# Seven quarter products for batch 1 as well, with the matrices for it prepared during batch 0

## The chip, the cores and the metric

One core of one Trainium2 chip runs the whole program. The time is that of the device, in microseconds (us), from start to end of one launch. TensorE (in the profile PE, its weight loads PEld) multiplies, VectorE (DVE) and ScalarE (ACT) work elementwise, GpSimd (POOL) does a little elementwise work, and SyncE (SP) issues nearly all transfers (DMA) from HBM.

## The reference

For each of 8 batches of 256 tokens (1024 channels), in float32:

```
w   = weight[adapter_ids[b]]              # 1024 x 1024, an adapter per batch
y   = x @ w.T                             # first product
out = x + y @ W_up.T + delta              # second product
# top1 = argmax(y @ gate_w.T + bias) over 4 experts
# delta = lora_B[top1] @ (lora_A[top1] @ y), rank 8
```

## The kernel before

**Numbers.** Each float32 operand is kept as a sum of two parts of lower precision, "hi" (ScalarE rounds, a CAST) and "lo" (VectorE subtracts hi from the raw number). A product is hi x hi + hi x lo + lo x hi: three matmuls.

**First product.** Per batch 8 blocks c of 128 output channels, block number n = 8b + c. TensorE runs block n into `ps_y[c % 2]`; ScalarE copies one half of it (`small`), VectorE adds the halves to `y_raw` (`y_full`). TensorE may begin block n only when `y_full` of block n - 2 is done. Meanwhile ScalarE and VectorE split W blocks ahead (`w_hi_part`, `w_lo_part`, three blocks ahead, `splits_at` and `splits_after` say which where), and SyncE loads W blocks into a ring of seven (`load_w`).

**Second product, in full.** Batches b < PLAIN = 2. y (256 x 1024) and W_up are each cut in four quarters; eight quarter products. The columns of lora_A and the gate ride along in the left quarters and give z and the logits. VectorE picks the expert (`choose`, a chain of small operations that ends in `z_parts`), TensorE transposes the result (`transpose_z`, ahead of the seventh of eight parts of the last quarter product), ScalarE copies it (`zT`), and TensorE adds the LoRA term (`add_lora`). VectorE adds the sums from PSUM onto the rows of x (`add_row`), and SyncE stores them.

**Second product, with seven quarter products.** Batches b >= PLAIN, by Strassen's scheme in Winograd's form: product 1 to 7 of sums of quarters of y (S1 to S4, by VectorE's `y_add`, split by `y_hi_part`, `y_lo_part`) with B11, B21, B22 and four sums of quarters of W_up, T1 to T4. These are made once: the raw quarters are copied from HBM again into the tiles `wide_stage` and `thin_stage`, summed (`t_raw`; the result stands in `wide_raw` or `thin_raw`), and split (`t_hi` on ScalarE, `t_lo` on VectorE). T1 and T4 are thin tiles, T2 and T3 wide ones. T4 uses the memory of B12, so its copies wait until the last product in full is done. In the kernel before T3 and T2 are summed in blocks 4 to 7 of batch 1's first product, T1 in its second, T4 in batch 2.

**Order.** There is no scheduler. Each engine has one program, written by hand, and runs it strictly in order; semaphores connect them. An instruction that waits holds up all behind it on its engine. SyncE's transfers too are issued in the program's order into one queue.

Of the kernel before, what the change touches and what calls it, by code (L numbers as in the profile page):

```python
# [8 lines left out]
ALU = mybir.AluOpType  # L9
# [16 lines left out]
def build(nc, xT, x, ids, w, w_up, gl, lora_b, bias, out):  # L26
# [22 lines left out]
    UNITS = 8  # L49
    PLAIN = 2  # L50
    QUART = HALF // 2
# [29 lines left out]
    with ExitStack() as ctx:  # L81
# [90 lines left out]
        up_ready = sem("up_ready")  # L172
        t_sum = sem("t_sum")
        t_hi_ready = sem("t_hi_ready")
        t_ready = sem("t_ready")
# [50 lines left out]

        T_ORDER = (T3, T1, T2, T4)

        def t_count(q, j):
            return 2 * T_ORDER.index(q) + j + 1  # L230

        SUM_ORDER = (T3, T2, T1, T4)

        def t_sum_count(q, j):
            return 2 * SUM_ORDER.index(q) + j + 1

        @block.sync
        def _(sp):
# [113 lines left out]
        @block.scalar  # L352
        def _(act):
# [23 lines left out]

            def t_hi(q):
                for j in range(2):
                    act.wait_ge(t_sum, t_sum_count(q, j))  # L380
                    act.copy(up_hi(q, pair(j)), up_raw(q, pair(j))).then_inc(t_hi_ready, 1)

# [25 lines left out]
            def first_product(b):  # L408
                for c in range(OC):
# [13 lines left out]
                    if (b, c) == (0, 5):  # L423
                        act.wait_ge(gl_in, 16)
                        gate_high(0)
                        gate_high(1)
                    if (b, c) == (1, 7):
                        t_hi(T3)
                    if (b, c) == (2, 3):
                        t_hi(T2)  # L430
                    if (b, c) == (2, 5):
                        t_hi(T4)

            def plain(b):
# [5 lines left out]
                if b == 0:  # L440
                    for u in UNITS_AFTER[1:]:
                        unit_hi(u)
                    constants()
                else:
                    t_hi(T1)
# [43 lines left out]
        def _(dve):  # L489
# [26 lines left out]
            def t_raw(q, j):  # L516
# [6 lines left out]
                elif q == T2:  # L523
# [88 lines left out]
            def first_product(b):  # L612
                for c in range(OC):
                    if c == OC - 1 and b >= PLAIN:
                        dve.wait_ge(y_full_ready, b * OC + c)
                        y_add(S2, A22, S3, ALU.subtract, slice(0, Q - 1))
                    y_full(b, c)
                    if c == 3 and b >= PLAIN:
# [12 lines left out]
                    if (b, c) in UNIT_AT:  # L631
                        unit_lo(UNIT_AT[b, c])
                    if b == 1 and c >= 4:
                        t_raw((T3, T2)[(c - 4) // 2], c % 2)
                    if b == PLAIN and c in (2, 3):
                        t_raw(T4, c - 2)
                    if b == PLAIN and c in (4, 5):
                        if c == 4:
                            dve.wait_ge(t_sum, t_sum_count(T4, 1))
                        t_lo(T2, c - 4)  # L640
                    if b == PLAIN and c == 6:
                        t_lo(T4, 0)

            def plain(b):
# [3 lines left out]
                y_lo_part(b, 4, A22)  # L648
                if b == 0:
                    for u in UNITS_AFTER[1:]:  # L650
                        unit_lo(u)
                    gate_low(2)
                    gate_low(3)
                    lora_b_lo()
                else:
                    for j in range(2):
                        t_raw(T1, j)
                    for j in range(2):
                        t_lo(T3, j)
                    for j in range(2):  # L660
                        t_lo(T1, j)
                for q in range(XQ):
# [13 lines left out]

            def strassen(b):
                dve.wait_ge(y_full_ready, (b + 1) * OC)
                y_add(S2, A22, S3, ALU.subtract, slice(Q - 1, Q))
# [11 lines left out]
                y_lo_part(b, 5, S1)  # L691
                y_lo_part(b, 6, A22)
                y_lo_part(b, 7, S4)
                dve.wait_ge(rows_in[1], (b + 1) * 16)
# [3 lines left out]
                add_row(b, 1, 0, out_cols(ps_v))  # L698
                if b == PLAIN:
                    t_lo(T4, 1)  # L700
                dve.wait_ge(product_done, products_before[b] + 3)
# [4 lines left out]
                add_row(b, 0, 1, out_cols(ps_u))  # L706
                if b + 1 < B:
                    x_lo(b + 1, 0)
                dve.wait_ge(product_done, products_before[b] + 4)
                dve.tensor_tensor(zg[:, 0, :], gate_out(ps_p), g_kept[:, 0, :], ALU.add).then_inc(g_step, 1)  # L710
                dve.wait_ge(g_step, gates_before[b] + 4)
                choose(b)
                if b + 1 < B:
                    x_lo(b + 1, 1)
                dve.wait_ge(product_done, products_before[b] + 5)
                add_row(b, 1, 1, ps_u[:, 0, :].rearrange("p (h n) -> p h n", h=2), after=5)
                if b == B - 1:

                    add_row(b, 0, 1, ps_u[:, 0, :].rearrange("p (h n) -> p h n", h=2), after=6)
                if b + 1 < B:  # L720
                    x_lo(b + 1, 2)
                    x_lo(b + 1, 3)
                for n in splits_after(b):
                    w_lo_part(n)
                lora_before = PLAIN * 4 + (b - PLAIN) * 4
                dve.wait_ge(out_done, lora_before + 1)
                add_row(b, 1, 1, ps_y[1][:, :].rearrange("p (h n) -> p h n", h=2), after=7)
                dve.wait_ge(out_done, lora_before + 2)
# [3 lines left out]
                dve.wait_ge(out_done, lora_before + 4)  # L732
                if b < B - 1:
                    dve.wait_ge(product_done, products_before[b] + 7)
# [29 lines left out]
        def _(pe):  # L764
# [103 lines left out]
            def product_thin(b, n, ps, p, q, start):  # L868
                for k in range(Q):
                    last = quarter(ps, p, q, k, start and k == 0, False)  # L870
                    if n == 6 and k == 1:
                        transpose_z(b)
# [11 lines left out]
            def strassen(b):  # L884
# [19 lines left out]
                pe.wait_ge(y_ready, y_before + 5)  # L904
                pe.wait_ge(row_step, rows_done + 6)
                product_thin(b, 5, ps_u[:, 0, :], S1, T1, True)
# [4 lines left out]
                product_thin(b, 6, ps_v[:, 0, :], A22, T4, True)  # L911
                pe.wait_ge(zt_ready, b * T + 2)
# [3 lines left out]
                if b < B - 1:  # L916
                    pe.wait_ge(row_step, rows_done + 7)
# [52 lines left out]
```

## Time and profile before

| | |
|---|---|
| median of 3 runs | 369.48 us (369.34 to 369.98) |
| the profiled execution | 369.84 us, span 368.1 us |
| PE | 363.1 us busy, 99% |
| DVE, ACT | 271.6 us (74%), 157.9 us (43%) |
| granted TensorE clock | 1.0 throughout |

The span runs from the first to the last instruction. A timeline row gives start and duration in us, the engine, the line in the kernel, operation, output <- inputs, shape, how many instructions were merged (x2), and in brackets how long the engine had been idle and what ended that. Where rows with x2 or more are merged, the duration is that of the group. In a row of windows each engine has its busy time and number of instructions.

### The profile page before, as it was taken

To read this page: it belongs to the slowest core of one execution; us is meant where nothing else is said; L and a number is where in the kernel's file an instruction comes from. 1 tells how busy PE (TensorE), PEld (TensorE's weight loads), DVE (VectorE), ACT (ScalarE), POOL (GpSimd) and SP (SyncE) were. 2 spreads that over 40 slices of the span, in tenths; PEclk is the share of its full clock that TensorE was granted. 3 is DMA by queue.
4 is the path that set the end of the run, shared out by engine and by line. 5 is a ranking of instruction groups with operands and counts; after the bars stand their busy time and mean duration, and the time that the engine had idled before them with its cause. 6 is when DMAs were issued, how large, how long until landed. Compare 5 with 4: busy or idle time off the path is not lost.

```text
span 368.1 us, 5953 instructions
## 1 busy us (share of the span) xinstructions
PE 363.1 (99%) x2193; PEld 325.2 (88%) x2193; DVE 271.6 (74%) x537; ACT 157.9 (43%) x315; POOL 1.8 (0%) x11
## 2 busy tenths in 40 slices
PE   7999999999999999999999999999999999999996
PEld 5888988899888998889988898888988899888995
DVE  4777847799478999678856788567984778856773
ACT  5677724645137533456025551155413553144300
POOL 0010000000000000000000000000000000000000
PEclk9999999999999999999999999999999999999999
DMA  7999984971079620686026750476404862160003
GB/s 246 396 401 307 405 318 174 325 251 51 0 274 330 223 89 2 250 319 232 0 116 234 267 187 2 170 264 211 157 0 180 325 213 85 49 238 0 3 0 114
DMA packets 20252, 68.16 MB, mean 185 GB/s; under 512 B 2304, under 2 KB 2688, under 8 KB 20224
## 3 DMA queue, kind: packets, MB, share of 16 engines
q1 hardware_dynamic: 19936, 66.74, 50.1%
q10 hardware_dynamic: 288, 1.05, 0.8%
q8 instruction: 17, 0.28, 0.3%
q14 instruction: 11, 0.09, 0.1%
HBM read 59.39 MB, written 8.39 MB: 184 GB/s over the span
## 4 chain that ended last, share of the span: by engine, by line
PE 99%; DVE 0%; issue 0%
PE ps_y L787 32%; PE ps_y L790 16%; PE ps_u L798 13%; PE ps_v L798 8%; PE ps_p L798 5%; PE ps_u L806 3%; PE ps_u L808 3%; PE ps_u L804 3%; PE ps_p L804 2%; PE ps_p L806 2%; PE ps_p L808 2%; PE ps_y L768 2%; PE ps_v L804 2%; PE ps_v L808 1%; PE ps_v L806 1%; PE ps_u L880 1%
## 5 line engine op out<-in xcount | busy, mean ns | idle before, releaser
L787 PE MATMUL ps_y<-x_hilo,w_hi 128*128 128x512 f32 x512 | 161.0, 396 | 0.0
L790 PEld LDWEIGHTS ps_y<-x_hilo,w_lo 128*128 128x128 f32 x512 | 96.2, 188 | 22.7
L790 PE MATMUL ps_y<-x_hilo,w_lo 128*128 128x256 f32 x512 | 100.6, 278 | 0.0
L506 DVE TENSOR_TENSOR w_lo<-w_raw,w_hi 128x512 fp32r<-128x512 f32 x126 | 81.6, 691 | 13.6 <-ACT w_hi L370 12.9
L787 PEld LDWEIGHTS ps_y<-x_hilo,w_hi 128*128 128x128 f32 x512 | 78.5, 189 | 0.9 <-DVE w_lo L499 0.4
L370 ACT CAST w_hi<-w_raw 128x512 fp32r<-128x512 f32 x126 | 71.8, 624 | 1.7 <-DMA w_raw<-w_dram 1.6
L385 ACT COPY small<-ps_y 128x256 f32<-128x256 f32 x64 | 23.9, 373 | 104.9 <-PE ps_y L790 104.9
L557 DVE TENSOR_TENSOR y_raw<-ps_y,small 128x256 f32<-128x256 f32 x64 | 27.1, 423 | 46.3 <-ACT small L385 46.3
L798 PE MATMUL ps_u<-wide_hi,y_parts 128*128 128x256 f32 (+1 forms) x256 | 47.2, 288 | 0.0
L798 PEld LDWEIGHTS ps_u<-wide_hi,y_parts 128*128 128x128 f32 x256 | 39.4, 188 | 1.4
L393 ACT CAST zT<-ps_y 128x128 fp32r<-128x128 f32 x16 | 3.5, 270 | 75.4 <-PE ps_y L814 75.4
L568 DVE TENSOR_TENSOR y_parts<-y_raw,y_parts 128x512 fp32r<-128x512 f32 x50 | 32.5, 686 | 1.3 <-ACT y_parts L388 0.9
L388 ACT CAST y_parts<-y_raw 128x512 fp32r<-128x512 f32 x50 | 28.9, 619 | 9.6 <-DVE y_raw L563 9.6
L798 PE MATMUL ps_v<-wide_hi,y_parts 128*128 128x256 f32 (+1 forms) x160 | 30.2, 289 | 0.0
L576 DVE TENSOR_TENSOR rows<-ps_u,rows 128x512 f32<-128x512 f32 x38 | 24.8, 682 | 4.8 <-issue 4.5
L798 PE MATMUL ps_u<-wide_lo,y_parts 128*128 128x256 f32 (+1 forms) x128 | 26.5, 288 | 0.0
L798 PEld LDWEIGHTS ps_v<-wide_hi,y_parts 128*128 128x128 f32 x160 | 24.6, 189 | 0.0
L493 DVE TENSOR_TENSOR x_hilo<-x_raw,x_hilo 128x512 fp32r<-128x512 f32 x32 | 20.9, 684 | 3.8 <-ACT x_hilo L357 3.5
L798 PEld LDWEIGHTS ps_u<-wide_lo,y_parts 128*128 128x128 f32 x128 | 20.6, 188 | 0.0
L357 ACT CAST x_hilo<-x_raw 128x512 fp32r<-128x512 f32 x32 | 17.9, 617 | 5.9 <-DMA x_raw<-xT_dram 5.8
L563 DVE TENSOR_TENSOR y_raw<-y_raw 128x512 f32<-128x512 f32 (+2 forms) x30 | 16.9, 581 | 0.4
L806 PE MATMUL ps_u<-thin_lo,y_parts 128*128 128x512 f32 x44 | 17.2, 390 | 0.0
(94 smaller groups left out, 386.0 us busy)
## 6 DMA issues: line engine op xcount, KB each, us to landing
w_raw<-w_dram SPq DMA_DIRECT2D x64, 512.0 KB, 4.7
rows<-x_dram SPq DMA_DIRECT2D x16, 512.0 KB, 5.9
out_dram<-rows SPq DMA_DIRECT2D x15, 512.0 KB, 2.7
x_raw<-xT_dram SPq DMA_DIRECT2D x14, 512.0 KB, 4.9
wide_raw<-w_up_dram SPq DMA_DIRECT2D x4, 512.0 KB, 11.2
thin_raw<-w_up_dram SPq DMA_DIRECT2D x4, 512.0 KB, 12.2
wide_stage<-w_up_dram SPq DMA_DIRECT2D x4, 512.0 KB, 13.9
thin_stage<-w_up_dram SPq DMA_DIRECT2D x4, 512.0 KB, 9.4
```

What stands on the lines that cost most here:

```text
L370: act.copy(w_hi[:, n % RING, part], w_raw[:, n % RAWS, part]).then_inc(w_hi_ready, QUARTERS // HALVES)
L385: act.copy(small[:, c % 2, :], ps_y[c % 2][:, S:2 * S]).then_inc(y_small_ready, 1)
L388: act.copy(y_parts[:, p, :, 0, :], y_raw[:, p, :, 1, :]).then_inc(y_hi_ready, 1)
L506: dve.tensor_tensor(w_lo[:, n % RAWS, part], w_raw[:, n % RAWS, part], w_hi[:, n % RING, part].bitcast(F32), ALU.subtract).then_inc(w_read ...
L557: dve.tensor_tensor(y_raw[:, p:p + 2, c % Q, 1, :], ps_y[c % 2][:, 0:S].rearrange("p (t n) -> p t n", t=T), small[:, c % 2, :].rearrange(" ...
L568: dve.tensor_tensor(y_parts[:, p, :, 1, :], y_raw[:, p, :, 1, :], y_parts[:, p, :, 0, :].bitcast(F32), ALU.subtract).then_inc(y_ready, 1)
L576: dve.tensor_tensor(row, ps, row, ALU.add).then_inc(row_step, 1)
L787: pe.matmul(ps_y[c % 2][:, :], w_hi[:, n % RING, i * P:(i + 1) * P], x_hilo[:, :, i, :], start=(i == 0), stop=False)
L790: last = pe.matmul(ps_y[c % 2][:, S:2 * S], w_lo[:, n % RAWS, i * P:(i + 1) * P], x_hilo[:, 0, i, :], start=False, stop=(i == KC - 1))
L798: last = pe.matmul(ps[:, h, 0:end - h * QUART], y_parts[:, p, k, y, :], up(q, k, slice(h * QUART, end)), start=start and n == 0, stop=stop ...
L804: pe.matmul(ps, y_parts[:, p, k, 0, :], up_hi(q, k), start=start, stop=False, skip_group_check=True)
L806: pe.matmul(ps, y_parts[:, p, k, 0, :], up_lo(q, k), start=False, stop=False, skip_group_check=True)
```

## The change

PLAIN becomes 1: batch 1 is the first with seven quarter products. What was prepared during batch 1 is prepared during batch 0 and batch 1's first product. The six copies for T3, T1 and T2 go ahead of most of batch 1's W blocks and its x. VectorE sums T3 and T2 in batch 0's second product; GpSimd sums T1, half by half, as soon as the halves of T2 are there; T4 is summed in blocks 1 and 2 of batch 1. Splits of all four follow in batch 1. In batch 1's second product product 7 comes ahead of the LoRA products, the transposes stand in product 7, and VectorE's order is another.

```diff
-    PLAIN = 2
+    PLAIN = 1
-        if c < OC - AHEAD or (b == 1 and c == 5) or (b > PLAIN and c < OC - 1):
+        if c < OC - AHEAD or (b > PLAIN and c < OC - 1):
...  # SyncE
-            i = load_blocks(OC, OC + RAWS - 1, i)
+            i = load_blocks(OC, OC + 2, i)
+            load_stage(T3, 0, 1)
+            load_stage(T1, 1, 1)
+            i = load_blocks(OC + 2, OC + 4, i)
+            load_stage(T2, 0, 0)
+            i = load_blocks(OC + 4, OC + RAWS - 1, i)
             load_x(1)
             i = load_blocks(OC + RAWS - 1, OC + RAWS, i)
             load_rows(0)
-            load_stage(T3, 0, 1)
-            load_stage(T1, 1, 1)
-            load_stage(T2, 0, 0)
...  # GpSimd
+            pool.wait_ge(stage_in[T1], 32)
+            for j in range(2):
+                pool.wait_ge(t_sum, t_sum_count(T2, j))
+                pool.tensor_tensor(up_raw(T1, pair(j)), up_stage(T1, pair(j)), up_raw(T2, pair(j)), ALU.subtract
+                                   ).then_inc(t1_sum, 1)
...  # ScalarE, first product
-                    if (b, c) == (1, 7):
-                        t_hi(T3)
-                    if (b, c) == (2, 3):
-                        t_hi(T2)
-                    if (b, c) == (2, 5):
-                        t_hi(T4)
+                    if b == PLAIN and 1 <= c < 5:
+                        t_hi((T3, T2)[(c - 1) // 2], (c - 1) % 2)
+                    if b == PLAIN and c in (5, 6):
+                        for j in range(2):
+                            t_hi((T1, T4)[c - 5], j)
...  # VectorE, first product
                     if c == OC - 1 and b >= PLAIN:
                         dve.wait_ge(y_full_ready, b * OC + c)
                         y_add(S2, A22, S3, ALU.subtract, slice(0, Q - 1))
+                        if b == PLAIN:
+                            t_lo(T1, 1)
                     y_full(b, c)
...
-                    if b == 1 and c >= 4:
-                        t_raw((T3, T2)[(c - 4) // 2], c % 2)
-                    if b == PLAIN and c in (2, 3):
-                        t_raw(T4, c - 2)
-                    if b == PLAIN and c in (4, 5):
...
-                        t_lo(T2, c - 4)
+                    if b == PLAIN and c in (1, 2):
+                        t_raw(T4, c - 1)
+                    if b == PLAIN and c == 4:
+                        t_lo(T3, 0)
+                    if b == PLAIN and c == 5:
+                        t_lo(T3, 1)
...
+                        t_lo(T2, 0)
                     if b == PLAIN and c == 6:
-                        t_lo(T4, 0)
+                        dve.wait_ge(t1_sum, 2)
+                        t_lo(T2, 1)
+                        t_lo(T1, 0)
...  # VectorE, second product in full
                 lora_b_lo()
+                for j in range(2):
+                    t_raw(T3, j)
+                    t_raw(T2, j)
                 for q in range(XQ):
                     x_lo(b + 1, q)
                 dve.wait_ge(z_done, b + 1)
...  # TensorE, strassen(b), first = b == PLAIN
+                if first:
+                    pe.wait_ge(row_step, rows_done + 7)
+                    pe.wait_ge(y_ready, y_before + 7)
+                    product_thin(b, 7, ps_u[:, 0, :], S4, B22, False)
                 pe.wait_ge(zt_ready, b * T + 2)
                 add_lora(b, 1, 1, ps_y[1][:, :], True)
```

In VectorE's `strassen` of batch 1 the remainders of A22 and S4 move behind the rows that they stood ahead of, T4's two remainders stand ahead of S4's, `choose` follows the row of product 5, and all four remainders of the next x follow `choose`.

On SyncE, from the copies of batch 1's W blocks on (`w_raw` a W block, `x_raw` batch 1's x, `wide_stage` and `thin_stage` the quarters for T3 and T2, and for T1; every ISA row only sets up the copy behind it), the order before and then the order now:

```order
L249 DMA w_raw<-w_dram 128x1024
L256 DMA x_raw<-xT_dram 128x1024 x2
L249 ISA
L249 DMA w_raw<-w_dram 128x1024
L272 DMA rows<-x_dram 128x1024 x2
L265 DMA wide_stage<-w_up_dram 128x2x512 x2
L265 DMA thin_stage<-w_up_dram 128x1024 x2
L265 DMA wide_stage<-w_up_dram 128x2x512 x2
```

And now, from block 9 on:

```order
L250 DMA w_raw<-w_dram 128x1024
L266 DMA wide_stage<-w_up_dram 128x2x512 x2
L266 DMA thin_stage<-w_up_dram 128x1024 x2
L250 ISA
L250 DMA w_raw<-w_dram 128x1024
L250 ISA
L250 DMA w_raw<-w_dram 128x1024
L266 DMA wide_stage<-w_up_dram 128x2x512 x2
L250 ISA
L250 DMA w_raw<-w_dram 128x1024
L250 ISA
L250 DMA w_raw<-w_dram 128x1024
```

The six copies moved from behind batch 1's x to ahead of it; x (line 257) follows directly behind the last row.

On VectorE in batch 0's second product, from the last operation on the constants to the first of the choice, before:

```order
L551 TENSOR_TENSOR lb_parts<-lb_raw,lb_parts 64x1024
L493 TENSOR_TENSOR x_hilo<-x_raw,x_hilo 128x512 x4
L665 COPY zg<-ps_u 128x36
L666 COPY zg<-ps_v 128x36
L587 TENSOR_TENSOR lg<-zg,bias_sb 128x8
```

The same place now (lines 528 and 533 are `t_raw` of T3 and of T2):

```order
L555 TENSOR_TENSOR lb_parts<-lb_raw,lb_parts 64x1024
L528 TENSOR_TENSOR wide_raw<-thin_stage,wide_stage 128x2x512
L533 TENSOR_TENSOR wide_raw<-wide_raw,wide_stage 128x2x512
L528 TENSOR_TENSOR wide_raw<-thin_stage,wide_stage 128x2x512
L533 TENSOR_TENSOR wide_raw<-wide_raw,wide_stage 128x2x512
L500 TENSOR_TENSOR x_hilo<-x_raw,x_hilo 128x512 x4
L670 COPY zg<-ps_u 128x36
```

Four sums came in ahead of the remainders of x; the choice still follows these.

On VectorE in the first batch with seven products, from block 4's W split to the remainder of S3 (`y_parts<-y_raw` splits a part of y, line 540 is `t_lo`), before:

```order
L506 TENSOR_TENSOR w_lo<-w_raw,w_hi 128x512 x2
L568 TENSOR_TENSOR y_parts<-y_raw,y_parts 128x4x128
L540 TENSOR_TENSOR wide_lo<-wide_raw,wide_hi 128x2x512
L557 TENSOR_TENSOR y_raw<-ps_y,small 128x2x128
L540 TENSOR_TENSOR wide_lo<-wide_raw,wide_hi 128x2x512
L557 TENSOR_TENSOR y_raw<-ps_y,small 128x2x128
L540 TENSOR_TENSOR thin_lo<-thin_raw,thin_hi 128x1024
L563 TENSOR_TENSOR y_raw<-y_raw 128x3x128
L557 TENSOR_TENSOR y_raw<-ps_y,small 128x2x128
```

The same place now (line 544 is `t_lo`):

```order
L544 TENSOR_TENSOR wide_lo<-wide_raw,wide_hi 128x2x512
L561 TENSOR_TENSOR y_raw<-ps_y,small 128x2x128
L544 TENSOR_TENSOR wide_lo<-wide_raw,wide_hi 128x2x512 x2
L561 TENSOR_TENSOR y_raw<-ps_y,small 128x2x128
L544 TENSOR_TENSOR wide_lo<-wide_raw,wide_hi 128x2x512
L544 TENSOR_TENSOR thin_lo<-thin_raw,thin_hi 128x1024
L567 TENSOR_TENSOR y_raw<-y_raw 128x3x128
L544 TENSOR_TENSOR thin_lo<-thin_raw,thin_hi 128x1024
L561 TENSOR_TENSOR y_raw<-ps_y,small 128x2x128
```

Six remainders of T stand there instead of three.

## Rows read from the trace of the kernel before

**Rows 1.** The page, part 4: the chain that ended last, by engine.

```profile
PE 99%; DVE 0%; issue 0%
```

**Rows 2.** Timeline of PE, the start: us, us, engine line op [idle before].

```profile
1.96 6.61 PE L768 MATMUL ps_y<-warm 128*128 128x512 f32 x18 [1.96 <-DVE warm L746]
```

**Rows 3.** Timeline of PE: each first matmul of batches 1, 2 and 3.

```profile
55.59 0.62 PE L787 MATMUL ps_y<-x_hilo,w_hi 128*128 128x512 f32 x2
...
102.17 0.61 PE L787 MATMUL ps_y<-x_hilo,w_hi 128*128 128x512 f32 x2
...
145.93 0.61 PE L787 MATMUL ps_y<-x_hilo,w_hi 128*128 128x512 f32 x2
```

**Rows 4.** Timeline of SP's queue, 24 to 44 us.

```profile
24.26 4.74 SPq L249 DMA_DIRECT2D w_raw<-w_dram  x6
31.31 0.81 SPq L256 DMA_DIRECT2D x_raw<-xT_dram  x2
...
33.65 3.20 SPq L265 DMA_DIRECT2D wide_stage<-w_up_dram  x2
...
40.25 3.46 SPq L265 DMA_DIRECT2D wide_stage<-w_up_dram  x2
```

**Rows 5.** Windows: busy of PE, PEld, DVE, ACT, POOL; PEclk, DMA share, GB/s.

```profile
28.00:30.00 2.00, 2.00 (x14) 1.73 (x13) 1.30 (x5) 1.32 (x2) 0.00 (x0) 1.00 1.00 187
...
34.00:36.00 2.00, 2.00 (x16) 1.91 (x15) 2.00 (x3) 2.00 (x4) 0.00 (x0) 1.00 1.03 412
...
50.00:52.00 2.00, 2.00 (x11) 1.65 (x10) 1.79 (x11) 0.00 (x0) 0.00 (x0) 1.00 1.03 400
```

**Rows 6.** Timeline of ACT, 41 to 45 us.

```profile
41.96 1.14 ACT L357 CAST x_hilo<-x_raw 128x512 fp32r<-128x512 f32 x2 [1.96 <-DMA x_raw<-xT_dram]
43.34 1.15 ACT L357 CAST x_hilo<-x_raw 128x512 fp32r<-128x512 f32 x2 [0.23 <-DMA x_raw<-xT_dram]
```

**Rows 7.** Timeline of DVE, 41 to 52 us.

```profile
41.25 1.22 DVE L551 TENSOR_TENSOR lb_parts<-lb_raw,lb_parts 64x1024 fp32r<-64x1024 f32 x1
42.61 2.68 DVE L493 TENSOR_TENSOR x_hilo<-x_raw,x_hilo 128x512 fp32r<-128x512 f32 x4
49.15 0.20 DVE L665 COPY zg<-ps_u 128x36 f32<-128x36 f32 x1 [3.86 <-PE ps_v L798]
...
51.34 0.36 DVE L609 TENSOR_TENSOR z_parts<-zm,z_parts 128x64 fp32r<-128x64 f32 x2
```

**Rows 8.** Timeline of PE, 52 to 53 us.

```profile
52.82 0.39 PE L808 MATMUL ps_p<-thin_hi,y_parts 128*128 128x512 f32 x1
53.05 0.33 PE L814 MATMUL ps_y<-eye,z_parts 128*128 128x128 f32 x2
```

**Rows 9.** Timeline of POOL; line 506 at 24.5 us, and in all.

```profile
24.05 0.95 POOL L349 TENSOR_TENSOR gl_raw<-gl_raw 128x144 f32<-128x144 f32 x1 [22.42 <-DMA gl_raw<-gl_dram]
...
L506 DVE TENSOR_TENSOR w_lo<-w_raw,w_hi x2: 692/842/991, 23.9 to 24.6; 128x512 fp32r<-128x512 f32 x2
...
L506 DVE TENSOR_TENSOR w_lo<-w_raw,w_hi x126: 680/687/991, 10.7 to 336.7; 128x512 fp32r<-128x512 f32 x126
```

**Rows 10.** Timeline of DVE in batch 2, and PE at its second product.

```profile
105.55 0.42 DVE L557 TENSOR_TENSOR y_raw<-ps_y,small 128x256 f32<-128x256 f32 x1 [0.92 <-ACT small L385]
...
108.33 0.42 DVE L557 TENSOR_TENSOR y_raw<-ps_y,small 128x256 f32<-128x256 f32 x1 [0.90 <-ACT small L385]
...
117.64 0.42 DVE L557 TENSOR_TENSOR y_raw<-ps_y,small 128x256 f32<-128x256 f32 x1
...
125.05 0.42 DVE L557 TENSOR_TENSOR y_raw<-ps_y,small 128x256 f32<-128x256 f32 x1 [0.66 <-ACT small L385]
...
125.84 0.69 DVE L568 TENSOR_TENSOR y_parts<-y_raw,y_parts 128x512 fp32r<-128x512 f32 x1
...
127.48 0.42 PE L798 MATMUL ps_v<-wide_hi,y_parts 128*128 128x256 f32 x2
```

**Rows 11.** Tile thin_stage, its copies.

```profile
DMA to landing us min/median/max: 3.7/9.4/13.7
```

More of the change, by code:

```diff
@@ L376, in unit_hi, with t_hi @@
                 act.copy(up_hi(q, ks), up_raw(q, ks)).then_inc(up_hi_ready, 1)
-            def t_hi(q):
-                for j in range(2):
+            def t_hi(q, j):
+                if q == T1:
+                    act.wait_ge(t1_sum, j + 1)
+                else:
                     act.wait_ge(t_sum, t_sum_count(q, j))
-                    act.copy(up_hi(q, pair(j)), up_raw(q, pair(j))).then_inc(t_hi_ready, 1)
+                act.copy(up_hi(q, pair(j)), up_raw(q, pair(j))).then_inc(t_hi_ready, 1)
             def y_small(b, c):
@@ L439, in plain @@
                 y_hi_part(A22)
[L440 to L445, printed above, removed]
+                for u in UNITS_AFTER[1:]:
+                    unit_hi(u)
+                constants()
                 for q in range(XQ):
@@ L648, in plain @@
                 y_lo_part(b, 4, A22)
[L649 to L661, printed above, removed]
+                for u in UNITS_AFTER[1:]:
+                    unit_lo(u)
+                gate_low(2)
+                gate_low(3)
+                lora_b_lo()
+                for j in range(2):
+                    t_raw(T3, j)
+                    t_raw(T2, j)
                 for q in range(XQ):
@@ L677, in strassen, with row_11_of_7, row_11_of_lora @@
             def strassen(b):
+                first, last = b == PLAIN, b == B - 1
+                lora_before = PLAIN * 4 + (b - PLAIN) * 4
+                def row_11_of_7():
+                    dve.wait_ge(product_done, products_before[b] + 5)
+                    add_row(b, 1, 1, ps_u[:, 0, :].rearrange("p (h n) -> p h n", h=2), after=5)
+                def row_11_of_lora():
+                    dve.wait_ge(out_done, lora_before + 1)
+                    add_row(b, 1, 1, ps_y[1][:, :].rearrange("p (h n) -> p h n", h=2), after=7)
                 dve.wait_ge(y_full_ready, (b + 1) * OC)
@@ L691, in strassen @@
                 y_lo_part(b, 5, S1)
-                y_lo_part(b, 6, A22)
-                y_lo_part(b, 7, S4)
+                if not first:
+                    y_lo_part(b, 6, A22)
+                    y_lo_part(b, 7, S4)
                 dve.wait_ge(rows_in[1], (b + 1) * 16)
@@ L706, in strassen @@
                 add_row(b, 0, 1, out_cols(ps_u))
-                if b + 1 < B:
+                if first:
+                    for j in range(2):
+                        t_lo(T4, j)
+                    y_lo_part(b, 7, S4)
+                elif not last:
                     x_lo(b + 1, 0)
@@ L710, in strassen @@
                 dve.tensor_tensor(zg[:, 0, :], gate_out(ps_p), g_kept[:, 0, :], ALU.add).then_inc(g_step, 1)
+                if first:
+                    row_11_of_7()
                 dve.wait_ge(g_step, gates_before[b] + 4)
                 choose(b)
-                if b + 1 < B:
+                if first:
+                    x_lo(b + 1, 0)
+                if not last:
                     x_lo(b + 1, 1)
-                dve.wait_ge(product_done, products_before[b] + 5)
-                add_row(b, 1, 1, ps_u[:, 0, :].rearrange("p (h n) -> p h n", h=2), after=5)
-                if b == B - 1:
+                if not first:
+                    row_11_of_7()
+                if last:
                     add_row(b, 0, 1, ps_u[:, 0, :].rearrange("p (h n) -> p h n", h=2), after=6)
-                if b + 1 < B:
+                else:
                     x_lo(b + 1, 2)
                     x_lo(b + 1, 3)
-                for n in splits_after(b):
+                splits = splits_after(b)
+                for n in splits[0:2]:
                     w_lo_part(n)
-                lora_before = PLAIN * 4 + (b - PLAIN) * 4
-                dve.wait_ge(out_done, lora_before + 1)
-                add_row(b, 1, 1, ps_y[1][:, :].rearrange("p (h n) -> p h n", h=2), after=7)
+                if first:
+                    row_11_of_lora()
+                for n in splits[2:]:
+                    w_lo_part(n)
+                if not first:
+                    row_11_of_lora()
                 dve.wait_ge(out_done, lora_before + 2)
@@ L732, in strassen @@
                 dve.wait_ge(out_done, lora_before + 4)
-                if b < B - 1:
+                if not last:
                     dve.wait_ge(product_done, products_before[b] + 7)
@@ L905, in strassen @@
                 pe.wait_ge(row_step, rows_done + 6)
+                if first:
+                    pe.wait_ge(t_ready, t_count(T1, 1))
                 product_thin(b, 5, ps_u[:, 0, :], S1, T1, True)
@@ L915, in strassen @@
                 add_lora(b, 1, 0, ps_v[:, 0, :])
[L916 removed]
+                if first:
+                    add_lora(b, 0, 1, ps_u[:, 0, :])
+                elif b < B - 1:
                     pe.wait_ge(row_step, rows_done + 7)
```

22 lines of the change are left out of this document (10 added, 12 removed).

## The prediction

> **What bounds the kernel now.** I read the chain of waits first. All of it is TensorE [rows 1], and TensorE waited only once, for the 2.0 us before its warm-up [rows 2]. So the time is TensorE's list of matmuls, and nothing taken off another engine can save anything. The change can act in two ways only: a shorter list, or a wait where there is none now. I then read where each batch's first matmul stands [rows 3]: 55.59, 102.17, 145.93 us. A batch multiplied in full costs 102.17 - 55.59 = 46.58 us, and one with seven quarter products 145.93 - 102.17 = 43.76 us. After that I looked for slack: when things that TensorE waits for are ready, against when it asks. This needs SyncE's queue [rows 4], the transfer rate [rows 5], and the three compute engines around 40 to 55 us [rows 6 to 8], where the preparation for batch 1 is moved to.
>
> **The matmuls.** Batch 1 goes from 46.58 to 43.76 us: -2.82 us. Its seventh product moves ahead of the LoRA products, and its two transposes from the sixth product to the seventh; the count of matmuls is that of batch 2 before. Batches 2 to 7 keep theirs. The sums and splits that batch 2 loses stood beside a busy TensorE and give nothing back.
>
> **The copies of w_up.** Before, the queue holds, from 24.26 us, the W blocks 8 to 13, then batch 1's x (two copies), W block 14, rows, and last the six copies for T3, T1, T2 [rows 4]. SyncE needs 3.2 to 3.5 us to issue two of these (0.8 us for x's two), so the queue is full and the rate of the transfers sets everything. They move 400 to 412 GB/s from 34 us on [rows 5], so a copy of 524,288 bytes takes 1.295 us at 405 GB/s. Afterwards all six copies stand ahead of x: 6 x 1.295 = 7.77 us later. ScalarE waited for x's first half until 41.96 and for its second until 43.34 us [rows 6]; these become 49.73 and 51.11 us.
>
> Who waits for x? ScalarE rounds it, VectorE takes the remainder, and VectorE does that *ahead of* batch 0's choice of the expert, in program order. The choice stood at 49.15 us, directly behind z [rows 7], since x had long been split. TensorE's transposes take its result at 53.05 us with no idle time before them [rows 8]; the choice ends at 51.34 + 0.36 = 51.70 us, so there are 1.35 us of slack. Now: x's second half 51.11, ScalarE's two roundings 1.15 [rows 6], VectorE's last remainder 0.80 later (45.29 against 44.49 us), so 53.06; the choice takes 51.70 - 49.15 = 2.55, so 55.61 us. TensorE waits 55.61 - 53.05 = 2.6 us by the transfers alone. VectorE's four sums (T3, T2 in halves) fit ahead of that if nothing disturbs them: the copies for T2 are the tenth from block 8 where x's first was the seventh, so they land at 41.96 + 3 x 1.295 = 45.85 us, and sums at 1.14 us a step (41.25 to 42.61 us shows one of 1.22 us and its follower) end at 49.4 us, before x.
>
> **T1 on GpSimd.** The trace has one comparable operation: GpSimd's subtraction of 128x144, from 24.05 to 25.00 us. VectorE's first half of w_lo, begun at 23.9 us, took 692 ns as always; the second, begun at 24.6 us, took 991 ns, where the median of all 126 is 687 ns [rows 9]. I read this as exclusion by turns: GpSimd waited for the running instruction, went in between two, and held the next up for 0.30 us, which is 2.1 ns for each of 144 elements. By elements, 128x1024 gives 1024 / 144 x 0.30 = 2.16 us of standstill for VectorE, twice. Bounds: 0.30 us each if it is a fixed price (then as good as nothing above the 2.6 us); 1024 / 144 x 0.95 = 6.8 us each if the whole operation counts, which I think too much since 0.6 us of the 0.95 passed while VectorE's first half ran undisturbed. I take 2.16, nearest to what VectorE's own row lost, and keep both ends for the range.
> The Trainium skill says, in SBUF — State Buffer, section "Who interferes with whom", that a VectorE instruction with two SBUF inputs and a GpSimd instruction that reads SBUF shut each other out for a whole instruction, in order of issue; this trace agrees, with the 991 ns. Its GPSIMD Engine Reference (section 3.1) gives 4497 ns for 2048 elements, an estimate of 2.2 us for 1024. If the engines shared instead of excluding each other, the sum would be the 2.6 us case.
>
> In order: T2's first half ends at 47.0, T3's second at 48.1 us; GpSimd, released at 47.0, goes in at 48.2 and out at 50.35; T2's second half ends at 51.5; the first remainder of x at 52.1; GpSimd's second goes in between and out at 54.3; three remainders at 0.60 a step end at 56.2; the choice at 58.75 us. TensorE's wait: 58.75 - 53.05 = 5.7 us. It replaces the 2.6, and is not added to it. Everything behind (w_lo of blocks 8 to 10, batch 0's rows) keeps its distance from the choice, about that of before (w_lo follows it directly; batch 1's first matmul comes 55.59 - 53.05 = 2.5 us behind the transposes), and costs nothing more.
>
> **TensorE's clock.** The granted clock is full throughout before [rows 5], so its price after a pause of 5.7 us is not to be read there. Bounds: nothing; or what the start cost, where after idleness 18 matmuls took 6.61 us [rows 2] instead of 18 x 0.23 = 4.1 us [rows 8], so 2.5 us. I take 2.5 for a pause this long, nothing for one of 2.6 us. The Trainium skill (TensorE: Matmul & The Clock Gate, part 1) says that idleness lowers the clock to 1.2 GHz and sustained work brings it back; no row of before shows a fall within the kernel. By that rule too the long pause pays and the short one probably not.
>
> **Batch 1 with VectorE's new work.** Batch 2 before is the pattern [rows 10]. Ahead of the last y_full VectorE gets four remainders more (T3, T1) and one less (T4's first): 3 x 1.14 = 3.4 us. T4's sums move a block earlier, into idle time, so the fifth y_full comes on time, at 105.55 + 4 x 2.78 = 116.67, instead of at 117.64 us: 0.95 back; and the 0.66 us of idle time before the last is used up. So the last y_full is late by 3.4 - 0.95 - 0.66 = 1.8 us. The remainder of S3 ended at 125.84 + 0.69 = 126.53, product 2 began at 127.48 us: 0.95 us of slack, so 0.85, with the semaphore 1.0 us of waiting. T1's halves (ScalarE at blocks 5 and 6) come from GpSimd some 15 us earlier and hold nothing up; T4's copies, issued at the end of batch 0, have 7 us where such a copy needs 3.7 us on an empty queue [rows 11]. The third to seventh product then have slack of 0.4 us and more, because the choice and x's remainders are put behind TensorE's needs; at the start of batch 2 VectorE is nearly 2 us behind, which TensorE's third block just bears: 0 to 0.3 us, taken as 0.
>
> **Sum.** -2.82 + 5.7 + 2.5 + 1.0 = +6.4 us. The profiled execution was timed at 369.84 us (span 368.1 and 1.7 around it): 376.2. It lies 0.36 us above the median of 369.48, so I predict 375.9 us.
>
> **Rivals.**
> (B) The exclusion happens, the clock stays: 369.48 + 3.9 = 373.4 us. For it: full clock in every row of before. Against: no pause like this is in them.
> (C) GpSimd costs VectorE nothing noticeable; only x is late. +0.8: 370.3 us. For it: one single row speaks for the exclusion, and the price could be fixed. The copies' arithmetic stands without it.
> (D) Faster: x isn't late enough. The place is the queue. If x's second half lands by 53.05 - 2.55 - 1.95 = 48.55 us, 5.2 us later than now rather than 7.8, the choice is in time, and with GpSimd cheap only the 1.0 in batch 1 is left: 367.7 us. For it: at 28 to 30 us the queue moves 187 GB/s and not 412 [rows 5], and copies could fill that time. Against: the same small copies still stand ahead and are passed in order.
> (E) GpSimd holds for longer than by elements, up to 6.8 us: 379 us and above.
>
> **Chances.** Forecast 0.42, B 0.18, C 0.16, D 0.15, E 0.09. Between D and C lies what a measurement can't tell from no change (0.2%, 0.74 us: 368.7 to 370.2); C's lower part falls there. Faster 0.15, same 0.08, slower 0.77. The range leaves out D and most of E: 369.9 to 379.0 us.
>
> **What would show it.** TensorE idle before batch 0's transposes, put down to VectorE's z_parts: 5.7 us (forecast), 2.6 (C), none (D). ScalarE's rounding of x starting near 49.7 and 51.1 us. Two GpSimd subtractions, each with a VectorE instruction beside it that takes 2 us more than its kind. A granted clock under 1.00 in the 5 us behind the pause (B: none). TensorE idle by 1.0 us before batch 1's second product. Batch 1 from first matmul to first matmul 43.8 + 1.0 us. If the choice still starts at 49.15 us, the main step is wrong; if GpSimd's two operations pass without a long VectorE instruction, the second is.

## The result and the profile after

The median of 4 runs is 377.08 us (376.47 to 378.64) against 369.48 us of the three runs of the kernel before (a fourth, of 729.24 us, is left out). The ratio is 1.0207 (95% interval 1.0195 to 1.022). The forecast was 375.9 us. The profiled execution took 377.01 us, span 375.2.

The page, parts 1, 2 and 4, of the kernel after (busy us and share; the granted clock in 40 slices; the chain by engine):

```profile
PE 362.9 (97%) x2180; PEld 324.6 (87%) x2180; DVE 282.3 (75%) x552; ACT 159.3 (42%) x318; POOL 7.3 (2%) x13
PEclk9999996999999999999999999999999999999999
PE 81%; SPq 6%; DVE 5%; DMA 5%; issue 2%; ACT 0%; DVEq 0%
```

TensorE holds the whole chain no longer [rows 1], and the clock has a dip in the seventh slice (56.3 to 65.7 us). Followed back from there, the chain runs over the choice, the remainders of x and VectorE's sums to the landing of T2's copies, and from there over SyncE's queue. The longest piece of the chain (start, us, what):

```profile
32.73 13.93 DMA wide_stage<-w_up_dram
```

Waits of TensorE (who waits <- for whom: us in all, times, longest):

```profile
PE ps_y L844 <- DVE z_parts L613: 6.2, 1, 6.2
PE ps_y L798 <- DVE warm L776: 2.0, 1, 2.0
PE ps_v L828 <- DVE y_parts L572: 0.9, 1, 0.9
```

The first and the last are new: the result of batch 0's choice, and the remainder of S3 for batch 1's second product. TensorE around the pause, and at the first matmul of batches 1 and 2, which answer to [rows 3, 8]:

```profile
59.33 0.69 PE L844 MATMUL ps_y<-eye,z_parts 128*128 128x128 f32 x2 [6.21 <-DVE z_parts L613]
...
64.19 0.76 PE L817 MATMUL ps_y<-x_hilo,w_hi 128*128 128x512 f32 x2
...
90.73 0.52 PE L828 MATMUL ps_v<-wide_hi,y_parts 128*128 128x256 f32 x2 [0.92 <-DVE y_parts L572]
...
109.27 0.62 PE L817 MATMUL ps_y<-x_hilo,w_hi 128*128 128x512 f32 x2
```

The transposes start 59.33 - 53.05 = 6.3 us later than before. From there to batch 1 it takes 64.19 - 59.33 = 4.9 us and not 2.5 [rows 3, 8]; batch 1 takes 109.27 - 64.19 = 45.1 us and not 46.6.

Why the choice is late is seen on VectorE (answers to [rows 7]), GpSimd and ScalarE (to [rows 6]):

```profile
46.68 1.23 DVE L533 TENSOR_TENSOR wide_raw<-wide_raw,wide_stage 128x1024 f32<-128x1024 f32 x1 [3.05 <-DMA wide_stage<-w_up_dram]
47.83 1.22 DVE L528 TENSOR_TENSOR wide_raw<-thin_stage,wide_stage 128x1024 f32<-128x1024 f32 x1
49.15 3.24 DVE L533 TENSOR_TENSOR wide_raw<-wide_raw,wide_stage 128x1024 f32<-128x1024 f32 x1
52.31 4.64 DVE L500 TENSOR_TENSOR x_hilo<-x_raw,x_hilo 128x512 fp32r<-128x512 f32 x4
56.87 0.18 DVE L670 COPY zg<-ps_u 128x36 f32<-128x36 f32 x1
```

```profile
48.06 3.25 POOL L357 TENSOR_TENSOR thin_raw<-thin_stage,wide_raw 128x1024 f32<-128x1024 f32 x1 [23.05 <-DVE wide_raw L533]
52.47 2.73 POOL L357 TENSOR_TENSOR thin_raw<-thin_stage,wide_raw 128x1024 f32<-128x1024 f32 x1 [1.17 <-DVE wide_raw L533]
```

```profile
50.52 2.43 ACT L365 CAST x_hilo<-x_raw 128x512 fp32r<-128x512 f32 x4 [10.61 <-DMA x_raw<-xT_dram]
```

T2's second half takes 3.24 us where the first took 1.23. GpSimd, begun at 48.06, is inside it until 51.31; four remainders of x take 4.64 us and not 2.68 [rows 7], with GpSimd's second operation inside. ScalarE gets x at 50.52 us. VectorE, still inside the sum of T2's second half until 52.39 us, isn't held up by x there: in this kernel the pause comes by T2's copies and GpSimd, and x alone would have made it about half as long (3.6 us in queue_only, 3.3 in pool_writes, both below). The choice starts at 56.87 instead of 49.15 us. The clock by windows (third column from the right):

```profile
57.00:58.00 1.00, 0.00 (x0) 0.00 (x0) 0.83 (x7) 0.00 (x0) 0.00 (x0) 0.82 0.00 0
58.00:59.00 1.00, 0.00 (x0) 0.00 (x0) 0.90 (x6) 0.00 (x0) 0.00 (x0) 0.50 0.00 0
...
64.00:65.00 1.00, 1.00 (x5) 0.82 (x5) 1.00 (x3) 0.00 (x0) 0.00 (x0) 0.77 0.00 0
65.00:66.00 1.00, 1.00 (x8) 0.87 (x7) 0.84 (x2) 0.00 (x0) 0.00 (x0) 1.00 0.52 127
```

It fell to 0.50 (1.2 of 2.4 GHz) during the pause and stayed there up to the first matmuls of batch 1. The pair of these takes 0.76 us and not 0.62 [rows 3].

### The profile page after: what moved, and what is told of

The parts are those of the page before. It is cut to its first block, busy times and chain, and to the rows that moved or that the text cites. A ratio compares the mean times of both kernels' runs of the same rounds, so it can differ in the third digit from the quotient of the medians.

```text
span 375.2 us, 5962 instructions
## 1 busy us (share of the span) xinstructions
PE 362.9 (97%) x2180; PEld 324.6 (87%) x2180; DVE 282.3 (75%) x552; ACT 159.3 (42%) x318; POOL 7.3 (2%) x13
## 4 chain that ended last, share of the span: by engine, by line
PE 81%; SPq 6%; DVE 5%; DMA 5%; issue 2%; ACT 0%; DVEq 0%
PE ps_y L817 27%; PE ps_y L820 13%; PE ps_u L828 10%; PE ps_v L828 6%; PE ps_p L828 6%; DMA wide_stage<-w_up_dram 4%; PE ps_u L836 3%; PE ps_u L834 3%; PE ps_u L838 3%; PE ps_v L834 2%; PE ps_v L838 2%; PE ps_v L836 2%; SPq L250 1%; SPq L241 1%; SPq L266 1%
## 5 line engine op out<-in xcount | busy, mean ns | idle before, releaser
L828 PE MATMUL ps_u<-wide_hi,y_parts 128*128 128x256 f32 (+1 forms) x256 | 46.2, 288 | 0.0
L828 PEld LDWEIGHTS ps_u<-wide_hi,y_parts 128*128 128x128 f32 x256 | 38.5, 188 | 0.7
L399 ACT CAST y_parts<-y_raw 128x512 fp32r<-128x512 f32 x53 | 30.6, 619 | 13.2 <-DVE y_raw L567 13.2
L572 DVE TENSOR_TENSOR y_parts<-y_raw,y_parts 128x512 fp32r<-128x512 f32 x53 | 34.6, 686 | 0.5
L580 DVE TENSOR_TENSOR rows<-ps_u,rows 128x512 f32<-128x512 f32 x43 | 28.1, 683 | 6.7 <-issue 5.6
L828 PE MATMUL ps_v<-wide_hi,y_parts 128*128 128x256 f32 (+1 forms) x144 | 26.6, 289 | 0.9 <-DVE y_parts L572 0.9
L500 DVE TENSOR_TENSOR x_hilo<-x_raw,x_hilo 128x512 fp32r<-128x512 f32 x32 | 23.0, 752 | 3.5 <-ACT x_hilo L365 3.4
L828 PEld LDWEIGHTS ps_v<-wide_hi,y_parts 128*128 128x128 f32 x144 | 21.8, 189 | 1.1 <-DVE y_parts L572 1.1
L834 PE MATMUL ps_u<-thin_hi,y_parts 128*128 128x512 f32 x52 | 20.3, 391 | 0.0
L836 PE MATMUL ps_u<-thin_lo,y_parts 128*128 128x512 f32 x52 | 20.3, 390 | 0.0
```

What stands on the lines that cost most here:

```text
L399: act.copy(y_parts[:, p, :, 0, :], y_raw[:, p, :, 1, :]).then_inc(y_hi_ready, 1)
L572: dve.tensor_tensor(y_parts[:, p, :, 1, :], y_raw[:, p, :, 1, :], y_parts[:, p, :, 0, :].bitcast(F32), ALU.subtract).then_inc(y_ready, 1)
L580: dve.tensor_tensor(row, ps, row, ALU.add).then_inc(row_step, 1)
L828: last = pe.matmul(ps[:, h, 0:end - h * QUART], y_parts[:, p, k, y, :], up(q, k, slice(h * QUART, end)), start=start and n == 0, stop=stop ...
L834: pe.matmul(ps, y_parts[:, p, k, 0, :], up_hi(q, k), start=start, stop=False, skip_group_check=True)
L836: pe.matmul(ps, y_parts[:, p, k, 0, :], up_lo(q, k), start=False, stop=False, skip_group_check=True)
```

## The experiments

All ten kernels stand in one table; the wait is TensorE's before batch 0's transposes, and "to batch 1" the time from the transposes to batch 1's first matmul in the profiled run. "Early" and "late" say whether batch 1's x stands ahead of T2's copies or behind them. Each ratio is to runs of the kernel before of the same round.

| kernel | x | T1 on | wait, us | to batch 1, us | median, us | ratio to before (95%) |
|---|---|---|---|---|---|---|
| before | early | | 0 | 2.5 | 369.5 to 369.9 | |
| the change | late | GpSimd | 6.2 | 4.9 | 377.08 | 1.0207 (1.0195 to 1.022) |
| queue_only | late | as before | 3.6 | 4.9 | 376.22 | 1.0174 (1.015 to 1.0198) |
| pool_writes | late | GpSimd, no reads | 3.3 | 4.9 | 374.17 | 1.0105 (1.0083 to 1.0128) |
| pool_half | late | GpSimd, half | 4.8 | 4.9 | 375.19 | 1.0142 (1.0125 to 1.0159) |
| t1_vector | late | VectorE | 4.0 | 4.2 | 373.02 | 1.0075 (1.0046 to 1.0104) |
| pause_filled | late | GpSimd | 0.9 | 2.7 | 374.81 | 1.0163 (1.0121 to 1.0204) |
| x_first_pool | early | GpSimd | 2.5 | 3.8 | 372.48 | 1.0065 (1.0043 to 1.0088) |
| x_first | early | VectorE | 0 | 2.6 | 368.40 | 0.9963 (0.995 to 0.9977) |
| x_first_t1_late | early | VectorE | 0 | 2.5 | 367.59 | 0.9936 (0.9923 to 0.995) |

**queue_only: the copies alone, in the kernel before.**

```diff
-            i = load_blocks(OC, OC + RAWS - 1, i)
+            i = load_blocks(OC, OC + 2, i)
+            load_stage(T3, 0, 1)
+            load_stage(T1, 1, 1)
+            i = load_blocks(OC + 2, OC + 4, i)
+            load_stage(T2, 0, 0)
+            i = load_blocks(OC + 4, OC + RAWS - 1, i)
             load_x(1)
```

> The kernel before with one thing changed: the six copies of w_up stand in the queue where the change puts them, ahead of batch 1's x. Theory (x late by itself makes TensorE wait, because the choice stands behind x's remainders): ScalarE gets x at 50.5 us as in the changed kernel, x is split by 53.4, the choice ends at 56.0, TensorE pauses 3.1 us before batch 0's transposes: 369.7 + 3.1 = 372.8 us if the clock stays, about 375 if it falls. Rival (the pause in the changed kernel comes from GpSimd and the new sums alone, the transfers are hidden): no pause, 369.7 us.

ScalarE, VectorE and TensorE in this kernel:

```profile
51.16 2.43 ACT L359 CAST x_hilo<-x_raw 128x512 fp32r<-128x512 f32 x4 [11.19 <-DMA x_raw<-xT_dram]
```

```profile
54.32 0.19 DVE L667 COPY zg<-ps_u 128x36 f32<-128x36 f32 x1
```

```profile
56.77 0.69 PE L816 MATMUL ps_y<-eye,z_parts 128*128 128x128 f32 x2 [3.59 <-DVE z_parts L611]
```

x comes at 51.2 us, the choice starts at 54.32, and TensorE pauses. So another order of the queue, without one operation more, makes the kernel slower by 6.4 us: the transposes start 56.77 - 53.05 = 3.7 us later, and half clock costs 2.3 us up to batch 1 and 0.3 in its first matmuls. The rival is out. The time is above the expected 375 or so: x came 0.7 us later than in the changed kernel, and so the pause was 3.6 and not 3.1 us. The half clock came with a pause of only 3.6 us, which the prediction had not expected.

**pool_writes: GpSimd writes and reads nothing.**

```diff
-                pool.tensor_tensor(up_raw(T1, pair(j)), up_stage(T1, pair(j)), up_raw(T2, pair(j)), ALU.subtract
-                                   ).then_inc(t1_sum, 1)
+                pool.memset(up_raw(T1, pair(j)), 1.0).then_inc(t1_sum, 1)
```

> The changed kernel, but GpSimd's two operations only write (a memset of the same tile, same waits and semaphores) and read nothing; T1 is wrong by that. Theory (two readers of SBUF shut each other out): VectorE's second half of T2 takes 1.2 us and not 3.2, x's four remainders 2.5 us and not 4.6; TensorE's pause is the 3.1 us of the transfers; 369.7 - 2.8 + 3.1 + 1.0 = 371.0 us with the clock up, up to 373.4 if it still falls. Rival (GpSimd costs nothing, x and the sums alone make the 6.3 us): 377.1 us as it was. Rival (any GpSimd operation on SBUF blocks, writing too): one long VectorE instruction each, near 377.

VectorE's rows and GpSimd's, of this kernel:

```profile
48.28 1.22 DVE L527 TENSOR_TENSOR wide_raw<-thin_stage,wide_stage 128x1024 f32<-128x1024 f32 x1
49.60 1.23 DVE L532 TENSOR_TENSOR wide_raw<-wide_raw,wide_stage 128x1024 f32<-128x1024 f32 x1
51.62 2.58 DVE L499 TENSOR_TENSOR x_hilo<-x_raw,x_hilo 128x512 fp32r<-128x512 f32 x4 [0.80 <-ACT x_hilo L364]
```

```profile
48.49 0.96 POOL L357 MEMSET thin_raw<- 128x1024 f32 x1 [24.66 <-DVE wide_raw L532]
```

GpSimd wrote from 48.49 to 49.45 us, inside VectorE's operation at 48.28 us, and that took its usual 1.22 us. So writing doesn't block here, reading does, and both long VectorE rows are GpSimd's reads. The wait is 3.3 us, near the 3.1 expected for the transfers. The time, 374.2 us, is above the 371.0 expected with the clock up and the 373.4 expected with it down: the clock fell again, and here the slow stretch reached further into batch 1, which took 45.6 us and not the change's 45.1.

**pool_half: half of the columns.**

```diff
-                pool.tensor_tensor(up_raw(T1, pair(j)), up_stage(T1, pair(j)), up_raw(T2, pair(j)), ALU.subtract
-                                   ).then_inc(t1_sum, 1)
+                pool.tensor_tensor(up_raw(T1, pair(j))[:, :, 0:QUART], up_stage(T1, pair(j))[:, :, 0:QUART],
+                                   up_raw(T2, pair(j))[:, :, 0:QUART], ALU.subtract).then_inc(t1_sum, 1)
```

Not shown: a memset fills T1 ahead of them, at 42.06 us, and three waits on `t1_sum` count one more for it.

> The changed kernel, but GpSimd subtracts only half of the columns of T1, twice 128x512; the rest of T1 is filled with a constant beforehand, so T1 is wrong. Theory (the price goes by elements, 2.2 ns each): VectorE's two standstills shrink from 2.1 to about 1.1 us each, the pause from 6.3 to about 4.4 us; 369.7 - 2.8 + 4.4 + 1.0 = 372.3 us with the clock up and 374.6 if it falls. Rival (a fixed price per operation): standstills and pause as before, 377.1 us.

```profile
49.68 2.13 DVE L535 TENSOR_TENSOR wide_raw<-wide_raw,wide_stage 128x1024 f32<-128x1024 f32 x1
51.73 3.57 DVE L502 TENSOR_TENSOR x_hilo<-x_raw,x_hilo 128x512 fp32r<-128x512 f32 x4
```

The standstill of T2's half is 2.13 - 1.23 = 0.9 us here and 3.24 - 1.23 = 2.0 us in the change: 1.8 to 2.0 ns per element, by elements and not by operation. The small subtraction of [rows 9] fits with its 2.1 ns. The wait was 4.8 and not 4.4 us, with x at 51.05 us, and the time, 375.2, is a little above the 374.6 us expected with the clock down.

**t1_vector: T1 on VectorE, all else as in the change.**

```diff
                 for n in splits_after(b):
                     w_lo_part(n)
+                    if n == OC:
+                        t_raw(T1, 0)
...
+                    if b == PLAIN and c == 0:
+                        t_raw(T1, 1)
```

Not shown: GpSimd's two operations go, and the order of the sums counts T1's halves.

> The changed kernel with T1 summed on VectorE: its first half behind block 8's W split, its second in block 0 of batch 1; GpSimd does nothing. All else, the queue too, as in the changed kernel, and the output is the reference's. Theory: TensorE's pause before the transposes shrinks from 6.3 to the 3.1 us of the transfers although VectorE now does 2.3 us more work; the wait at batch 1's second product stays 1.0 us: 371.0 us with the clock up, 373.4 with it down. Rival (VectorE's load and not the exclusion is what counts): 377 us or more.

4.1 us faster than the change, although VectorE does two operations of 1.22 us more. The wait was 4.0 and not 3.1 us; ScalarE got x at 51.35 us in this execution. The two profiled executions are 3.1 us apart: the transposes start 59.33 - 56.96 = 2.4 us earlier, and the slow stretch costs 0.8 us less. The eight runs spread from 370.43 to 374.75 us, the profiled one with the clock at 0.50 for most of the way from 57 to 61 us. In the two fastest, 370.43 and 370.76 us, the mean granted clock was 1.0, close to the 371.0 us expected with the clock up; in the slowest it was 0.991. So whether TensorE is slow behind such a pause, and for how long, varies from run to run.

**pause_filled: TensorE kept busy in the pause.**

```diff
                     if c == Q + 2:
+                        if b == 0:
+                            for _ in range(24):
+                                pe.matmul(ps_y[0][:, :], warm[:, 0:P], warm[:, :], start=True, stop=True)
                         transpose_z(b)
```

> The changed kernel with 24 matmuls of 128x512 on constants (a PSUM bank that is free then) put ahead of batch 0's transposes, so that TensorE works through most of its pause: 24 x 0.23 = 5.5 of 6.3 us. Theory (the half clock behind the pause costs 2.3 us of its own): the transposes still start near 59.3 us, the granted clock stays at 1.00, the rest of batch 0 takes 2.5 us and not 4.9: 377.1 - 2.4 = 374.7 us. Rival (the slow stretch comes from something else): 377.1 us.

```profile
52.88 5.60 PE L888 MATMUL ps_y<-warm 128*128 128x512 f32 x24
59.37 0.46 PE L844 MATMUL ps_y<-eye,z_parts 128*128 128x128 f32 x2 [0.88 <-DVE z_parts L613]
...
62.04 0.61 PE L817 MATMUL ps_y<-x_hilo,w_hi 128*128 128x512 f32 x2
```

The transposes begin where they did, but batch 1 follows 62.04 - 59.37 = 2.7 us later and not 4.9. The granted clock is 1.00 in every window from 52 to 68 us. The medians differ by 2.3 us; the prediction had taken 2.5 from the kernel's start [rows 2]. One of the four runs took 378.19 us at a mean clock of 0.994, so the clock fell somewhere in it too; no trace shows where. In the other three, useless work in a pause that couldn't be avoided was worth its clock.

**x_first: x ahead of T2's copies and of W blocks 9 to 14, T1 on VectorE.**

```diff
-            i = load_blocks(OC, OC + 2, i)
+            i = load_blocks(OC, OC + 1, i)
             load_stage(T3, 0, 1)
             load_stage(T1, 1, 1)
-            i = load_blocks(OC + 2, OC + 4, i)
+            load_x(1)
             load_stage(T2, 0, 0)
-            i = load_blocks(OC + 4, OC + RAWS - 1, i)
-            load_x(1)
-            i = load_blocks(OC + RAWS - 1, OC + RAWS, i)
+            i = load_blocks(OC + 1, OC + RAWS, i)
...
                 for j in range(2):
                     t_raw(T3, j)
-                    t_raw(T2, j)
                 for q in range(XQ):
                     x_lo(b + 1, q)
+                for j in range(2):
+                    t_raw(T2, j)
```

> t1_vector with batch 1's x ahead of T2's copies and of W blocks 9 to 14 (queue: block 8, T3, T1, x, T2, blocks 9 to 14), and VectorE's order in batch 0 T3, T3, remainders of x, T2, T2, choice. The output is the reference's. Theory (the pause is x's place in the queue alone): x at about 42 to 43.5 us, the choice starts near 49.2 to 49.7 us and is done before TensorE's 53.0, no pause, clock up; the 1.0 us at batch 1's second product stays: 369.7 - 2.8 + 1.0 = 367.9 us. Rival (VectorE is simply overloaded by T1 to T3 in batch 0 and 1, with waits elsewhere): 369.7 us or more, with new waits of TensorE in batch 1 and at the start of batch 2.

```profile
42.42 2.36 DVE L516 TENSOR_TENSOR wide_raw<-thin_stage,wide_stage 128x1024 f32<-128x1024 f32 x2
44.70 2.49 DVE L488 TENSOR_TENSOR x_hilo<-x_raw,x_hilo 128x512 fp32r<-128x512 f32 x4
47.11 2.35 DVE L521 TENSOR_TENSOR wide_raw<-wide_raw,wide_stage 128x1024 f32<-128x1024 f32 x2
49.38 0.19 DVE L663 COPY zg<-ps_u 128x36 f32<-128x36 f32 x1
```

All four sums fit, but for 0.2 us, into time in which VectorE had waited before [rows 7]: the choice starts at 49.38 us, and the wait is gone. The 0.9 us at the second product are left. The time, 368.4 us, is 0.5 above the expected 367.9. This edit moves several things at once (x, T2's copies, the W blocks and VectorE's order), so it shows that the pause can be avoided, and not which of them does it. That a late x is enough to make a pause is shown by queue_only.

**x_first_t1_late: in addition T1's splits out of the way of the last y_full.**

```diff
-                        if b == PLAIN:
-                            t_lo(T1, 1)
...
-                        t_lo(T1, 0)
...
                 y_lo_part(b, 3, S2)
+                if first:
+                    t_lo(T1, 0)
...
                 if first:
+                    t_lo(T1, 1)
                     for j in range(2):
                         t_lo(T4, j)
```

> x_first with T1's two splits moved from ahead of batch 1's last y_full to behind the remainder of S2 and behind product 3's rows. The output is the reference's. Theory (the wait at the second product comes from the splits that stand ahead of the last y_full): that wait goes, T1 is still in time for product 5 (34.4 us behind the batch's start, by my ledger met within 0.3 us), block 2 of batch 2 may wait 0.2 us: 366.9 to 367.4 us. Rival (VectorE's work is conserved, the wait moves to product 5 or 6): 367.9 us as x_first.

```profile
PE ps_y L792 <- DVE warm L770: 2.0, 1, 2.0
PE ps_u L828 <- DVE thin_lo L536: 0.3, 1, 0.3
```

The wait at the second product is gone; 0.3 us came back at product 5, where the ledger had said it would be met within 0.3. 367.59 us, 0.2 above the expected range: faster than the kernel before by 0.64% (interval 0.5% to 0.77%), than the changed one by 9.5 us, and than x_first by 0.8 us.

**x_first_pool: the fourth case of the two switches.** x_first with T1 on GpSimd, whose two lines are those of the change; queue and VectorE's order are x_first's.

> x_first, but T1 is summed on GpSimd as in the changed kernel; the output is the reference's. It is the fourth case of two switches (x early or late, T1 on GpSimd or VectorE). Theory (GpSimd's price is independent of the transfers): VectorE has T2 done at 49.4 us, GpSimd's two subtractions then fall into the choice, whose operations read two operands of SBUF, and hold it up by 2.2 us each; the choice ends near 56.2 and not 51.8 us, TensorE pauses about 3.3 us, 369.9 - 2.8 + 3.3 + 0.9 = 371.3 us with the clock up and up to 374 with it down. Rival (GpSimd costs time only where x is late too; small operations slip through between): 368.4 us as x_first.

```profile
49.40 0.18 DVE L670 COPY zg<-ps_v 128x36 f32<-128x36 f32 x1
49.61 2.04 DVE L589 TENSOR_TENSOR lg<-zg,bias_sb 128x8 f32<-128x8 f32 x1
51.69 0.16 DVE L591 TENSOR_REDUCE lmax<-lg 128x2 f32<-128x8 f32 x1
51.88 2.10 DVE L592 TENSOR_TENSOR top<-lg,lmax 128x8 f32<-128x8 f32 x1
54.02 0.17 DVE L594 TENSOR_TENSOR score<-top,rank 128x8 f32<-128x8 f32 x1
```

```profile
48.39 5.58 POOL L355 TENSOR_TENSOR thin_raw<-thin_stage,wide_raw 128x1024 f32<-128x1024 f32 x2 [24.23 <-DVE wide_raw L531]
```

An operation on 8 elements took 2.04 us, another 2.10, where they take 0.17. The copy from PSUM and the reduction, with one operand each, passed at 0.18 and 0.16 us. So GpSimd's price doesn't hang on x being late. The wait was 2.5 us and not 3.3; 372.5 us lies between the two values expected for the two clocks. The four cases together: T1 on GpSimd costs 377.08 - 373.02 = 4.1 us with x late and 372.48 - 368.40 = 4.1 us with x early, and x late costs 4.6 us with either. Both prices contain what the slow clock adds.

## Why the prediction was right

The term table of the sum, in us of the profiled executions:

| term | forecast | measured |
|---|---|---|
| seven products in batch 1 | -2.82 | -2.56: batch 1 took 45.08 us, 0.92 of it waiting and 0.14 lost to half clock, so 44.02 against 46.58 |
| later start of the transposes | 5.7 | 6.28, of which 6.21 are recorded as waiting |
| half clock behind it | 2.5 | 2.32, and 0.14 in batch 1's first matmuls |
| wait at the second product | 1.0 | 0.92 |
| sum | 6.4 | 7.1 (spans 375.2 and 368.1) |

**The copies.** Right in place and order, also in that the pause comes by the sums of T2 and GpSimd and replaces the one that x alone would make. x came 0.8 us later than by count of copies (50.52 against 49.73 us), and T2's copies by as much (46.68 against 45.85). That is most of what the wait was longer. Why six copies of w_up cost more than 1.295 us each here isn't settled; in queue_only, pool_writes, pool_half and t1_vector x came at 51.0 to 51.4 us. By x alone the forecast had a wait of 2.6 us; without GpSimd's reads it was 3.3 to 4.0.

**GpSimd.** The step was built on one row of 0.30 us [rows 9], read as exclusion by turns and scaled by elements to 2.16 us. Measured: 2.0 us for T2's half, and 4.64 - 2.49 = 2.15 us for x's remainders. The 2.16 was a choice between bounds of 0.30 and 6.8 us, and it came out. pool_writes shows that it is reading, pool_half that it goes by elements, x_first_pool that it stops even the smallest operation with two operands. The Trainium skill (SBUF — State Buffer, "Who interferes with whom") says the first, that a VectorE instruction with two SBUF inputs contends with a GpSimd instruction that reads SBUF and not with one that only writes it; this case's rows agree, with 3.24 us beside a reading one and 1.22 beside a writing one.

**The clock.** The size was right and the condition wrong: the forecast charged 2.5 us for a long pause, "nothing for one of 2.6 us", and read the rule that it cites in the same way. The clock fell with waits of 3.3, 3.6 and 4.0 us, and in x_first_pool, with a wait of 2.5 us, it fell just before 57 us and stayed down until after 60, when TensorE had been working again since 55.56. That the size agrees is in part luck. The 2.5 us were what matmuls at the kernel's start had lost, and the price here depends on how long the slow stretch lasts: with what batch 1 took above x_first's 44.9 us it was 2.5 us in the change, 3.0 in pool_writes and 1.7 in t1_vector and x_first_pool. Rival C (late x alone, 370.3 us) was for this reason too cheap: pool_writes, which is that case, took 374.17 us.

**Batch 1.** Without its wait and the slow clock it took 44.0 us where batch 2 before took 43.8; 0.3 us are not assigned. The ledger of VectorE's work gave 1.0 us, 0.9 was measured, and x_first_t1_late shows the splits ahead of the last y_full to be its cause.

**Where the gain is.** The change as an idea was worth having. What undid it was the order of one queue, and two operations on GpSimd that VectorE could do for less. With both mended the kernel is 0.37% faster than before (x_first), and 0.64% with T1's splits moved as well (x_first_t1_late).

## What to carry to other kernels

A kernel whose chain is all one engine has slack that the shares on its page don't show; before transfers are moved ahead in a queue, follow what they overtake through each engine's program order to the engine that sets the time. An elementwise operation of two operands on GpSimd costs VectorE nearly twice what VectorE would need for it itself (2.1 against 1.14 us for 128x1024), unless VectorE is idle, or reads one operand only, in the meantime (of the last these runs show only three operations of 0.2 us). A pause of TensorE costs itself and in most of these runs a slow stretch behind it, of 1.7 to 3.0 us here: count both, and where it can't be avoided, try to fill it.

## What the runs showed of the hardware that was not expected

- The granted clock can fall when the pause is over. Windows of x_first_pool, whose transposes start at 55.56 us:

```profile
56.00:57.00 1.00, 1.00 (x6) 0.82 (x5) 0.86 (x3) 1.00 (x4) 0.00 (x0) 0.95 0.00 0
57.00:58.00 1.00, 1.00 (x5) 0.81 (x4) 1.00 (x2) 1.00 (x3) 0.00 (x0) 0.50 0.00 0
```

  TensorE (second number) was at work in both, and the clock fell just before 57 us. In every profiled execution with a wait of 2.5 to 6.2 us ahead of the transposes it went to 0.50; in two of t1_vector's eight runs the mean clock stayed at 1.0.
- Behind the same kind of pause the slow stretch differs in length: from the transposes to batch 1 it took 4.9 us in four kernels, 4.2 in t1_vector and 3.8 in x_first_pool, and t1_vector's runs spread over 4.3 us while the eleven of the kernel before in the same round stay within 0.6 us.
- VectorE at 2.04 us for 128x8 stands for an operation that takes 0.17 us in other runs; the rest is GpSimd's subtraction. Such a row is read by looking for what another engine does at that time.
